# DLRM tower: all Gram matrices made sample by sample, with one VectorE transpose each

## What is computed

```python
e = jnp.stack([tbl_0[ids[:, 0]], ..., tbl_31[ids[:, 31]]], axis=1)      # (2048, 32, 128)
dot_products = jnp.einsum('bfd,bgd->bfg', e, e)
iu, ju = jnp.triu_indices(32, k=1)
z = dot_products[:, iu, ju]                                             # (2048, 496)
h = jnp.concatenate([z, dense_ctx], axis=1)                             # (2048, 512)
h = jnp.maximum(h @ W_top1 + b_top1, 0.0)                               # 512
h = jnp.maximum(h @ W_top2 + b_top2, 0.0)                               # 256
y = h @ W_top3                                                          # (2048, 1)
```

## Time and profile before

| what | value |
|---|---|
| time, median of 3 runs | 441.08 us (440.25 to 441.61) |
| span of the profiled execution | 437.2 us |
| its own time | known by its span; the median lies 3.9 us above it |
| TensorE busy | 395.3 us (90%) |
| TensorE weight loads busy | 366.9 us (84%) |
| VectorE busy | 337.8 us (77%) |
| ScalarE busy | 123.5 us (28%) |
| GpSimd (issuing gathers) busy | 309.1 us (71%) |
| mean granted TensorE clock | 0.992 of full |

### The profile page before, as it was taken

The page is one execution under the profiler, slowest core; times in us unless marked ns, Lnnn a source line. Parts: engine busy times, 40 slices in busy tenths (PEclk is TensorE's granted clock), DMA queues, the critical chain, the costliest instruction groups (busy, mean ns, idle before and its releaser), DMA issues.

```text
span 437.2 us, 11476 instructions
## 1 busy us (share of the span) xinstructions
PE 395.3 (90%) x4564; PEld 366.9 (84%) x4564; DVE 337.8 (77%) x873; ACT 123.5 (28%) x220; POOL 309.1 (71%) x324
## 2 busy tenths in 40 slices
PE   0467787999999999999999999999999999999967
PEld 0456687989989999898989999998989999998757
DVE  2599999997689949898689949897689949890510
ACT  1335410232214321332214220342214221432313
POOL 5777877777777777777777777777777777777300
PEclk9989999899999999999999999999999999999999
DMA  7999964525232532334252423335242442232100
GB/s 129 240 231 223 236 159 80 101 82 110 63 89 76 105 88 71 79 91 97 65 101 71 105 77 78 78 90 105 58 99 75 102 78 72 79 80 55 30 4 0
DMA packets 31293, 42.09 MB, mean 96 GB/s; under 512 B 11076, under 2 KB 24140, under 8 KB 31272
## 3 DMA queue, kind: packets, MB, share of 16 engines
q1 hardware_dynamic: 18936, 20.64, 22.3%
q0 software_dynamic: 10240, 20.99, 18.6%
q10 hardware_dynamic: 2096, 0.17, 0.4%
HBM read 41.77 MB, written 0.01 MB: 96 GB/s over the span
## 4 chain that ended last, share of the span: by engine, by line
PE 56%; DVE 30%; issue 4%; SPq 4%; DMA 4%; ACT 1%; DVEq 0%; ACTq 0%
DVE onehot L616 21%; PE sel_ps L290 20%; PE gram_ps L309 12%; PE work_ps L343 11%; DVE pairs L627 8%; PE work_ps L351 6%; PE work_ps L272 4%; DMA x<-tables_selected 3%; PE work_ps L416 2%; DVE table_lo L650 1%; SPq L217 1%; SPq L222 1%; PE work_ps L425 1%; SPq L197 1%; PE work_ps L326 1%
## 5 line engine op out<-in xcount | busy, mean ns | idle before, releaser
L243 POOL DMA_INDIRECT gathered<-table,tile_ids x320 | 308.9, 965 | 100.4 <-issue 95.7
L616 DVE TENSOR_SCALAR onehot<-id_rows,row_no 128x256 fp32r<-128x256 int32 x768 | 239.6, 387 | 12.7 <-DMA id_rows<-ids_selected 10.9
L290 PE MATMUL sel_ps<-onehot,table_hi 125*128 125x256 f32 x768 | 196.8, 295 | 32.5 <-DVE table_lo L650 17.0
L290 PE MATMUL sel_ps<-onehot,table_lo 125*128 125x256 f32 x768 | 190.0, 286 | 0.0
L290 PEld LDWEIGHTS sel_ps<-onehot,table_hi 125*128 125x128 f32 x768 | 148.9, 194 | 39.6 <-DVE table_lo L650 17.0
L290 PEld LDWEIGHTS sel_ps<-onehot,table_lo 125*128 125x128 f32 x768 | 149.3, 194 | 0.0
L627 DVE STREAM_TRANSPOSE pairs<-gram_ps 32x1024 f32<-32x1024 f32 x60 | 74.8, 1246 | 55.6 <-PE gram_ps L309 55.0
L475 ACT ACTIVATE rows_T<-sel_ps 128x512 f32<-128x512 f32 x48 | 30.0, 628 | 136.6 <-PE sel_ps L290 103.5
L309 PEld LDWEIGHTS gram_ps<-rows_T 128*64 128x64 f32 x1920 | 58.1, 140 | 4.7 <-issue 4.7
L466 ACT ACTIVATE rows_T<-work_ps 128x512 f32<-128x512 f32 x80 | 45.5, 598 | 56.7 <-PE work_ps L272 56.7
L309 PE MATMUL gram_ps<-rows_T 128*64 128x64 f32 x1920 | 60.2, 224 | 0.0
(11 more groups left out here) (26 smaller groups left out, 86.6 us busy)
## 6 DMA issues: line engine op xcount, KB each, us to landing
id_rows<-ids_selected SPq DMA_DIRECT2D x48, 256.0 KB
gathered<-table,tile_ids POOLq DMA_INDIRECT x320
pairs<-tables_selected SPq DMA_DIRECT2D x6, 448.0 KB
x<-tables_selected SPq DMA_DIRECT2D x6, 448.0 KB
w_sb<-w SPq DMA_DIRECT2D x1, 1024.0 KB
w_sb<-w SPq DMA_DIRECT2D x1, 512.0 KB
pairs<-tables_selected SPq DMA_DIRECT2D x6, 52.0 KB
x<-tables_selected SPq DMA_DIRECT2D x6, 52.0 KB
```

The lines of the kernel that those rows point to most:

```text
L243: nc.gpsimd.indirect_dma_start(gathered[:, t, g, :], None, tables_gathered[g], bass.IndirectOffsetOnAxis(ap=slot_id, axis=0)).then_inc(chu ...
L290: last_op = nc.tensor.matmul(sel_ps[:, u % 2, e, :], part[0:SEL_P, 2 * u + e, k, :], onehot[0:SEL_P, (2 * u + h) % HALF_SLOTS, kk, e, :], ...
L616: last_op = nc.vector.tensor_scalar(onehot[:, (2 * u + h) % HALF_SLOTS, kk, e, :], id_rows[:, slot, e, :], row_no[:, k:k + 1], None, ALU.i ...
```

## The change

All grams are made as the last one was: one sample a matmul, 32 columns by 32, in four column groups, into half of `gram_ps` (the half of its tile), and one VectorE transpose of 128 partitions turns it. TensorE's wait before a gram is on `gram_read` of the same tile of the pair before, since the tiles have halves of their own. `gram_part`, `doubles` and the 32-partition transposes go.

```diff
--- before.py
+++ after.py
@@ -128,11 +128,7 @@
         def layer_ps(bank, n):
             return work_ps[:, bank, 2 * n:2 * n + 2, :].rearrange("p a s -> p (a s)")
 
-        def doubles():
-
-            return gram_ps[:, :].rearrange("p (s a g) -> p s a g", a=2, g=N_FEAT)
-
-        def singles(t):
+        def samples(t):
 
             return gram_ps[:, t * P * N_FEAT // 4:(t + 1) * P * N_FEAT // 4].rearrange("p (s g) -> p s g", g=N_FEAT)
 
@@ -296,26 +292,17 @@
             def gram_waits(i, o, t):
                 pe.wait_ge(chunk_moved, at(i, o, 2 * NC, NC * (t + 1)))
                 pe.wait_ge(sel_moved, at(i, o, UNITS, UNITS))
-                if not (known_first(i, o) and t == 0):
-
-                    pe.wait_ge(gram_read, at(i, o, 2, t))
-
-            def gram_part(t, first, n):
-
-
-                for s in range(first, first + n):
-                    for j in range(2):
-                        rows = rows_T[:, t, 4 * s + 2 * j:4 * s + 2 * j + 2, :].rearrange("p a g -> p (a g)")
-                        last_op = nc.tensor.matmul(gram_ps[64 * j:64 * j + 64, 64 * s:64 * s + 64], rows, rows,
-                                                   start=True, stop=True)
-                return last_op
-
-            def gram_singles(t):
+                if not known_first(i, o):
+
+                    pe.wait_ge(gram_read, at(i, o - 1, 2, t + 1))
+
+            def gram(t):
+
 
                 for s in range(P // 4):
                     for j in range(4):
                         rows = rows_T[:, t, 4 * s + j, :]
-                        last_op = nc.tensor.matmul(singles(t)[32 * j:32 * j + 32, s, :], rows, rows,
+                        last_op = nc.tensor.matmul(samples(t)[32 * j:32 * j + 32, s, :], rows, rows,
                                                    start=True, stop=True)
                 last_op.then_inc(gram_done, 1)
 
@@ -374,7 +361,7 @@
                     pe.wait_ge(chunk_moved, at(i, o, 2 * NC, 5 + m))
                     layer1(i, o - 1, m)
                 gram_waits(i, o, 0)
-                gram_part(0, 0, 32).then_inc(gram_done, 1)
+                gram(0)
                 turn(i, o, 6)
                 turn(i, o, 7)
 
@@ -386,13 +373,13 @@
                 for cc in ((), (0,), (1, 2), (3, 4), (5,), (6, 7))[u]:
                     turn(0, 0, cc)
             gram_waits(0, 0, 0)
-            gram_part(0, 0, P // 4).then_inc(gram_done, 1)
+            gram(0)
             select(0, 1, 0)
             turn(0, 0, 8)
             turn(0, 0, 9)
             select(0, 1, 1)
             gram_waits(0, 0, 1)
-            gram_part(1, 0, P // 4).then_inc(gram_done, 1)
+            gram(1)
             pe.wait_ge(weights_in, 80)
             with pe.Fori(0, n_pairs - 2) as i:
                 to_first_gram(i, 1)
@@ -404,7 +391,7 @@
                 pe.wait_ge(chunk_moved, at(i, 1, 2 * NC, 9))
                 layer2(i, 0)
                 gram_waits(i, 1, 1)
-                gram_part(1, 0, 32).then_inc(gram_done, 1)
+                gram(1)
 
                 layer3(i, 0)
 
@@ -446,7 +433,7 @@
             pe.wait_ge(y_ready, last)
             turn_pairs(0, last, 0, 0)
             gram_waits(0, last, 1)
-            gram_singles(1)
+            gram(1)
             layer1_tile(0)
 
             turn_pairs(0, last, 1, 0)
@@ -618,20 +605,10 @@
                                                               ALU.is_equal)
                     last_op.then_inc(onehot_ready, 1)
 
-            def turn_gram(i, o, t, q):
-
-                if q == 0:
-
-                    dve.wait_ge(gram_done, at(i, o, 2, t + 1))
-                quadrant = slice(32 * q, 32 * q + 32)
-                last_op = nc.vector.transpose(pairs[quadrant, t, :, :],
-                                              doubles()[quadrant, :, q % 2, :].rearrange("p s g -> p g s"))
-                if q == 3:
-                    last_op.then_inc(gram_read, 1)
-
-            def turn_gram_singles(i, o, t):
+            def turn_gram(i, o, t):
+
                 dve.wait_ge(gram_done, at(i, o, 2, t + 1))
-                nc.vector.transpose(pairs[:, t, :, :], singles(t).rearrange("p s g -> p g s")
+                nc.vector.transpose(pairs[:, t, :, :], samples(t).rearrange("p s g -> p g s")
                                     ).then_inc(gram_read, 1)
 
             def merge_pairs(i, o, t):
@@ -654,8 +631,7 @@
 
             def to_first_gram(i, o):
 
-                for q in range(4):
-                    turn_gram(i, o - 1, 1, q)
+                turn_gram(i, o - 1, 1)
                 compare(i, o, 3, (1,))
                 merge_pairs(i, o - 1, 1)
                 compare(i, o, 4)
@@ -665,8 +641,7 @@
 
                 compare(i, o + 1, 0)
                 compare(i, o + 1, 1, (0,))
-                for q in range(4):
-                    turn_gram(i, o, 0, q)
+                turn_gram(i, o, 0)
                 compare(i, o + 1, 1, (1,))
                 merge_pairs(i, o, 0)
                 compare(i, o + 1, 2)
@@ -686,10 +661,9 @@
                 to_first_gram(i, 1)
                 gram0_and_next(i, 1)
             to_first_gram(0, last)
-            for q in range(4):
-                turn_gram(0, last, 0, q)
+            turn_gram(0, last, 0)
             merge_pairs(0, last, 0)
-            turn_gram_singles(0, last, 1)
+            turn_gram(0, last, 1)
             merge_pairs(0, last, 1)
 
 # ---- launch: one core; inputs and outputs as the reference has them ----
```

## The result

The changed kernel took 455.71 us in the median of its first four runs (452.3 to 459.2) against 440.66 for the kernel before; the ratio is 1.033 (95% interval 1.028 to 1.037), so it is **slower by about 15 us**. Its runs differ more than those of the kernel before: six later ones lie between 442.73 and 466.76 us, while the kernel before stays within 437.98 and 441.78 beside them. Ratios count only runs within 1.5% of the fastest of their kernel, here three of the four and two of the six, with 1.015 (1.008 to 1.021) for the latter, so that the change is a loss in every run but of no fixed size. The experiments tell where the loss comes from, and explain its spread in part.

The account below looks back on a forecast made before the run. TensorE was taken to pace the loop, with POOL's gathers capping any gain at 2.3 us; 28.9 + 2.5 - 2.6 + 0.9 = +29.7 on a 437.2 us span gave 466.9, plus 3.9 for the median: 471 us, range 438.5 to 480.

Parts of the forecast that it names:

- Bound of the loop: Loop: TensorE, busy 48.52 of 48.90 us a pass, sets the pace and covers VectorE's work.
- the step: Transposes in the loop: VectorE's saving of 7.5 us a pair is covered by TensorE; only 0.38 us a pass goes.
- POOL's limit on any gain: Gathers end about 2.5 us before their use, so no gain ahead of the last gram exceeds about 2.3 us.
- Grams of 2.59 us: New grams without holes cost 2.59 us, saving 1.29 each and 2.58 a pass; read from the last gram.
- Code in blocks, eight and nine: TensorE's code comes in 256-instruction blocks; the new loop touches eight, fetches a ninth, and nine don't fit; overflow chance 0.75.
- Every pass refetched: Loop: all blocks thrown out in turn, each pass fetched again, +28.9 us over five jumps back; chance 0.45.
- 2.5 for the clock: Low clock that may follow the hole at each jump back: 0 to 8.5 us, taken as 2.5.
- The rival of one lost block: Loop: only the first block is lost, grams stay 2.59 us in later passes; +8, 449 us; chance 0.30.
- Jump back 4.4 us: Loop's end: the jump finds no code fetched ahead and waits 3.1 to 6.2 us, taken as 4.4.
- First part -2.6 us: Prologue and first pass: first layer 1 gains 4.4 us from VectorE's saving and avoided low clock, less 1.76 lost.
- Tail +0.9: After the loop: the tail's first gram costs 0.88 us more, the last is unchanged.

Follow-up runs that it names:

- The two runs on VectorE's part: Four transposes a gram on the kernel with 100 waits: 452.55 us; one transpose a gram on the kernel before, second samples not turned: 437.21 us.
- the kernel with 100 waits: Changed kernel with 100 already met waits before TensorE's first select, so the loop's code touches seven blocks instead of eight: 440.39 us, ratio 1.001.
- 80 waits: Changed kernel with 80 already met waits before TensorE's first select; eighth code block entered 103 instructions before the jump back: 503.17 us, ratio 1.145.
- 240 waits: Changed kernel with 240 already met waits before TensorE's first select; eighth code block entered seven instructions before the jump back: 454.74 us, before 439.74.
- the run with few gathers: Kernel before with ten gathers a pair instead of 40 from the second pair on, on the slow chip: a pass 47.72 us, from 48.88.
- the run with VectorE relieved: Kernel before, each gram turned by one transpose of 128 partitions, the second samples' turning left out: 437.21 us, ratio 0.992.

## Why the prediction was right or wrong

- **Bound of the loop.** In part wrong. I took TensorE for the pace of the pass and VectorE for covered, because TensorE was busy 48.52 of 48.90 us. But the record of a select lasts 0.28 us and the next one starts after 0.12, so that busy time papers over short waits for the one-hot rows. The two runs on VectorE's part give 1.3 us (48.88 to 47.60) and 2.0 us (49.5 to 47.5) a pass, where the step had 0.38.
- **POOL's limit on any gain.** Right in kind. With one transpose on the old grams TensorE does end up waiting for gathers, and of 1.3 us a pass and 4.5 in the prologue only 3.3 us are left at the end (2.1 to 4.8 by the interval); the limit was put at 2.3.
- **Grams of 2.59 us.** Wrong in the loop. The last gram, from which the row came, is the only one made when no gather is under way. With gathers it is 3.3 to 4.1 us in the kernel with 100 waits, 3.7 on average, hardly better than the old 3.88. Read start to start, without the matmuls' latency, the undisturbed gram is even shorter, 2.29.
- **Code in blocks, eight and nine.** Right, down to the counts: clusters are nine packets, the hole in the second gram comes 249 of 256 records in, where the 24 instructions worked out for the eighth block put it at 250, and 20 already met waits are worth 63 us (503.17 less 440.39). What the prediction could only argue from seven shown blocks, the runs show: eight are kept (with 240 waits passes two to four touch eight and have no packet).
- **Every pass refetched.** Wrong, and the largest miss in the sum: 5 x (1.38 + 4.4) and 2.5 for the clock, 31.4 us, were charged for five refetched passes, and the profile has two clusters, which cost 6.2 and 7.6 us over the kernel before; with the last interval's -0.9 that is 12.9. The price forecast for one (5.8, or 6.3 with the clock) was near that. Where all five are refetched, with 80 waits, it is 11.7 over before: the hole for the second block was in no term. The rival of one lost block didn't occur: a cluster is nine packets. That a block has one fixed place, or that the oldest makes room, no run shows.
- **Jump back 4.4 us.** Measured 4.01 and 4.19, and 3.71 with 80 waits. The clock did fall after it, at both jumps with a miss (0.64 from 191.4 to 197.2 us, 0.69 from 294.5 to 300). No run shows the forecast's 2.5 us for it over five jumps: the 32 selects behind these two take 5.75 and 5.02 us against 3.92 without a hole, 2.9 us for two jumps.
- **First part -2.6 us.** Wrong sign. It was 4.4 gained by the first layer 1 and 1.76 lost in the first pass; measured are +3.5 and +3.0, together +6.5. The 3.46 us for a block came from the tail, where the DMA engines are busy to 0.02 (415 to 424 us, before); among the loads of the prologue, with DMA at 0.57 (62.0 to 71.2 us, after), the first gram alone had holes of 3.00 and 2.51 us and a clock of 0.71, and took 9.3 us (62.05 to 71.39) instead of 4.76. With old grams there layer 1 starts at 102.74. VectorE's share of the term was right: with old grams and one transpose layer 1 starts at 98.29, 4.5 us earlier than before; what of it an avoided low clock is worth no run shows.
- **Tail +0.9.** +0.6, right.

The forecast of 471 us was twice as far from before as the result; the direction and the range held. It was right on the cause and wrong on how often it strikes. Part of the closeness is luck: the refetched passes were put 18 us too high and the first part 9 us too low, and the two errors work against each other. Had all five passes been refetched at the 6.9 us a cluster of the profiled run, the median would have been some 483 us (an estimate: 437.2 + 5 x 6.9 + 6.5 + 0.6 + 3.9), and with 80 waits it is 503; both are above the range.

## What to carry to other kernels

Before a loop is made longer by shorter instructions, count its instructions and where its blocks begin: this loop took 503.17 us with 80 waits in front and 440.39 with 100, 20 instructions further, and the changed kernel fetched at different places in two runs (its second cluster from 290 us in one profile, from 343 in the other). Read the price of a short operation where the neighbours of its new place are at work too, not in the tail: 2.59 us there, 3.7 in the loop. TensorE was busy for 99% of a pass (48.52 of 48.90 us) and still waited for VectorE; the run with VectorE relieved told (47.60).

## What was not expected of the hardware

- While POOL issues gathers, TensorE's issue stops for 0.25 us on average, mostly 0.4 or 1.1 to 1.2 us after a gather's start (46 of the 48 gaps of 0.11 to 0.28 us that the starts of the changed kernel's matmuls show inside its grams from 134 to 400 us). The new grams, at 9 ns a record, feel it (3.84 us with all gathers, 2.29 with few, the first of a pass); the old ones, at 30 ns, don't (3.88 with both).
- One-hot comparisons on VectorE take 386 ns with all gathers and 351 ns with a quarter of them, 35 ns on each of 96 a pass or 3.4 us of VectorE's time, beside a pass of the old kernel that is 1.16 us shorter. The chip of the run with few gathers was another one; in the new kernel, on one chip, it is 387 and 355 ns.

```profile
L616 DVE TENSOR_SCALAR onehot<-id_rows,row_no 128x256 fp32r<-128x256 int32 x456 | 142.0, 386 | 0.8 <-DMA id_rows<-ids_selected 0.3
```

```profile
L616 DVE TENSOR_SCALAR onehot<-id_rows,row_no 128x256 fp32r<-128x256 int32 x485 | 133.3, 351 | 5.2 <-DMA id_rows<-ids_selected 4.7
```

- The loop is not fetched again in every pass: clusters came in five of five passes where the eighth block was entered 103 instructions before the jump, in two of five at 24 and in one of five at seven. That the closeness of the jump decides it is my reading of the packets and not shown by itself.
- With the new grams and four transposes a pass is 49.5 us, 0.6 longer than before. The 0.6 lies in TensorE's waits for one-hot rows, 2.0 us a pass there against 1.3 before; why they grow is open.
